# Edge sums with one-hots of 32 columns in four column groups of TensorE

## The reference

```python
m = x[src] * rel[edge_type]
m = concatenate([m[:half] @ W_in, m[half:] @ W_out])
deg = segment_sum(ones(e), dst); norm = 1 / maximum(deg, 1)
agg = segment_sum(m * norm[dst][:, None], dst)
out = tanh(agg + x @ W_loop + b)
```

## Time and profile before

| | |
|---|---|
| time, median of 3 runs (lowest, highest) | 1939.32 us (1937.36, 1941.78) |
| span of the profiled execution, first to last instruction | 1937.8 us |
| the execution's own time | not listed apart from its span; the span is 1.5 us below the median of the runs |
| PE busy | 1821.0 us, 94% of the span |
| POOL busy | 1322.3 us, 68% |
| DVE busy | 1248.8 us, 64% |
| ACT busy | 632.8 us, 33% |

### The profile page before, as it was taken

How to read it: one execution, slowest core, us unless ns; L and a number is a source line. 1 busy time by engine, 2 the same in 40 slices (tenths; PEclk the granted TensorE clock), 3 DMA queues, 4 the chain that set the end, 5 groups by cost and what they waited for, 6 DMA issues and landing times.

```text
span 1937.8 us, 28847 instructions
## 1 busy us (share of the span) xinstructions
PE 1821.0 (94%) x9176; PEld 1505.8 (78%) x9176; DVE 1248.8 (64%) x3345; ACT 632.8 (33%) x1552; POOL 1322.3 (68%) x1301
## 2 busy tenths in 40 slices
PE   2899899999899999999999789998899999999999
PEld 1567787887588888768888667876788888888998
DVE  6786465674855576486466645868765666654766
ACT  4452233343323333332333222332121211223443
POOL 6777777777777777777777757777777777770000
PEclk9999999999999999999999989999999999999999
DMA  9568666667776666687677856667766766661000
GB/s 274 177 198 258 203 191 206 186 202 222 243 209 199 204 194 198 208 249 214 193 218 220 274 190 229 190 200 224 229 182 215 209 199 200 190 181 17 15 28 28
DMA packets 194575, 371.44 MB, mean 192 GB/s; under 512 B 37993, under 2 KB 126095, under 8 KB 194430
## 3 DMA queue, kind: packets, MB, share of 16 engines
q0 software_dynamic: 77632, 223.91, 40.6%
q1 hardware_dynamic: 92228, 126.68, 19.9%
q10 hardware_dynamic: 24570, 19.04, 3.4%
HBM read 305.39 MB, written 64.95 MB: 191 GB/s over the span
## 4 chain that ended last, share of the span: by engine, by line
PE 80%; DVE 8%; issue 3%; DMA 3%; POOL 2%; SPq 2%; ACT 2%; DVEq 0%; ACTq 0%
PE ps_down L2765 16%; PE ps_hid L2753 16%; PE ps_seg L2629 15%; PE ps_kv L2662 5%; PE ps_x L2717 4%; PE ps_x L546 3%; PE ps_hid L3229 2%; PE ps_kv L3082 2%; POOL xg L959 2%; PE ps_hid L2682 1%; DVE xg L1055 1%; PE ps_kv L2795 1%; PE ps_down L2795 1%; DMA h_rows<-qT_all 1%; PE ps_hid L3220 1%
## 5 line engine op out<-in xcount | busy, mean ns | idle before, releaser
L959 POOL DMA_INDIRECT xg<-h_rows,idx_tab x416 | 437.2, 1051 | 143.3 <-issue 114.0
L906 POOL DMA_INDIRECT rg<-relation_rows,idx_tab x416 | 426.7, 1026 | 133.5 <-issue 126.1
L959 POOL DMA_INDIRECT xg<-xn_rows,idx_tab x416 | 423.4, 1018 | 131.9 <-issue 120.3
L2629 PE MATMUL ps_seg<-xg,hot 128*125 128x257 f32 x1664 | 414.8, 382 | 19.7 <-DVE xg L1055 19.5
L2753 PE MATMUL ps_hid<-hT,wff 128*128 128x250 f32 (+1 forms) x1920 | 368.3, 341 | 1.0 <-issue 0.8
L2629 PEld LDWEIGHTS ps_seg<-xg,hot 128*125 128x125 f32 x1664 | 305.3, 188 | 75.0 <-DVE xg L1055 19.2
L2765 PE MATMUL ps_down<-wff,gT 128*125 128x256 f32 x1600 | 363.6, 381 | 0.0
L2753 PEld LDWEIGHTS ps_hid<-hT,wff 128*128 128x128 f32 x1920 | 312.8, 189 | 37.9 <-issue 7.9
L1055 DVE TENSOR_TENSOR xg<-xg,rg 128x512 f32<-128x512 f32 x416 | 285.8, 687 | 70.8 <-DMA rg<-relation_rows,idx_tab 52.0
L2765 PEld LDWEIGHTS ps_down<-wff,gT 128*125 128x125 f32 x1600 | 295.2, 188 | 41.3
L2204 ACT ACTIVATE gT<-ps_hid,b1p 128x250 f32<-128x250 f32 (+1 forms) x480 | 177.8, 433 | 291.6 <-PE ps_hid L2753 291.5
(11 more groups left out here) (378 smaller groups left out, 2385.5 us busy)
## 6 DMA issues: line engine op xcount, KB each, us to landing
second_relation_rows<-rg SPq DMA_DIRECT2D x104, 512.0 KB, 4.1
rg<-second_relation_rows SPq DMA_DIRECT2D x104, 512.0 KB, 4.1
wff<-L_mix_W ACTq DMA_DIRECT2D x8, 1024.0 KB
rg<-relation_rows,idx_tab POOLq DMA_INDIRECT x416, 3.5
xg<-xn_rows,idx_tab POOLq DMA_INDIRECT x416, 3.2
xg<-h_rows,idx_tab POOLq DMA_INDIRECT x416, 3.6
h_rows<-qT_all SPq DMA_DIRECT2D x25, 112.0 KB
qrow<-h_rows ACTq DMA_DIRECT2D x25, 112.0 KB
```

The source lines that it names most:

```text
L906: pool.indirect_dma_start(rg[:, k, :], None, rel_d, bass.IndirectOffsetOnAxis(ap=idx_tab[:, step, 1:2], axis=0))\
L959: pool.indirect_dma_start(xg[:, k, 0:D], None, rows, bass.IndirectOffsetOnAxis(ap=idx_tab[:, step, 0:1], axis=0))\
L2629: ins = pe.matmul(ps_seg[u // UW % 2][0:T, 0:AW], hot[:, s % HOTS, :], xg[:, s % RING, :], start=s % WIN == 0, stop=s % WIN == WIN - 1)
```

## The change

One-hots become 32 columns wide in place of 125. The steps of a window are reordered so that step s of it goes to column group s modulo 4: two steps that follow each other in the sorted list share a group, and their destinations fit in 32 rows. PE takes a quad of four steps (two units) at a time: each step's product has 32 output rows, and the four go to the four groups of 32 columns of the array and of PSUM rows (`tile_position`). After the two quads of a window, the bank holds four blocks of 32 rows. DVE makes a placing one-hot (`placed`, from the new `place_tab`) and copies the bank to SBUF (`step_sums`; `copy_sums`, at the second unit of the next window); PE multiplies the two into the same bank (`place_sums`, after the next window's first quad), which puts each row where it stood before; then DVE does both adds, at the fourth unit instead of the third and fourth. `s_seg` moves by two units at a time, and a unit left over at a mark waits on PE for the next mark. The tables at the start gain `pair_pick`, `pair_first`, `place_tab` and a few more, and lose the step that shifted keys to their tile.

```diff
 STORE_AT = (2, 5)
 CUT = 112
 AHEAD = 6
+SPAN = 32
+COLS = P // SPAN
+QUAD = COLS
 
 
 
...
@@ -181,7 +184,10 @@
         xg = sb("xg", [EP, RING, AW])
         rg = sb("rg", [EP, RING, 2 * D])
         rg2 = rg[:, :, :].rearrange("p r (h d) -> p (r h) d", h=2)
-        hot = sb("hot", [EP, HOTS, T])
+        hot = sb("hot", [EP, HOTS, SPAN])
+        step_sums = sb("step_sums", [P, AW])
+        placed = sb("placed", [P, T])
+        place_tab = sb("place_tab", [P, WINS])
         iota_t = sb("iota_t", [EP, T])
...
+            pool.affine_select(out=pair_pick, in_=pair_pick, compare_op=ALU.not_equal, fill=1.0, base=0,
+                               pattern=[[-2, SCH // 2], [0, 2]], channel_multiplier=1)
...
+                            p(dve.tensor_copy(spread_steps(idx_tab[:, :, m]), by_groups(ps_tab[2 * m][0:EP, 0:STEPS2])))
...
@@ -1022,10 +1047,16 @@
                     self.rows = row, nc.s_assert_within((row < last_row) + row, min_val=0, max_val=last_row,
                                                         skip_runtime_bounds_check_because="one more only below the last")
 
+                def copy_sums(self, w):
+
+                    dve.tensor_scalar(placed[:, :], iota_t[:, :], place_tab[:, w:w + 1], None, ALU.is_equal)
+                    dve.wait_ge(s_seg, self.g * UNITS + (UW * (w + 1) + RU))
+                    dve.tensor_copy(step_sums[:, :], ps_seg[w % 2][:, 0:AW]).then_inc(s_cps, 1)
+
                 def add(self, w, m):
 
                     if m == 0:
-                        dve.wait_ge(s_seg, self.g * UNITS + (UW * (w + 1) + RU))
+                        dve.wait_ge(s_plc, self.g * WINS + w + 1)
                     dve.wait_ge(s_acc, (self.g * WINS + w) * 2 + (m + 3))
                     if self.scaled:
                         dve.wait_ge(s_sc, self.g * NB + self.scaled)
...
@@ -1041,10 +1072,11 @@
                         self.row_numbers(k // UW - 1)
                     at = k * UNIT
                     s = at % RING
-                    hs = at % HOTS
-                    dve.wait_ge(s_seg, g * UNITS + (k + 1 + RU - HOTS // UNIT))
-                    dve.tensor_tensor(hot[:, hs:hs + UNIT, :], iota_t[:, :].unsqueeze(1).broadcast_to([EP, UNIT, T]),
-                                      key_tab[:, at:at + UNIT].unsqueeze(2).broadcast_to([EP, UNIT, T]), ALU.is_equal)
+                    if at % QUAD == 0:
+                        hs = at % HOTS
+                        dve.wait_ge(s_seg, g * UNITS + (k + QUAD // UNIT + RU - HOTS // UNIT))
+                        dve.tensor_tensor(hot[:, hs:hs + QUAD, :], iota_t[:, 0:SPAN].unsqueeze(1).broadcast_to([EP, QUAD, SPAN]),
+                                          key_tab[:, at:at + QUAD].unsqueeze(2).broadcast_to([EP, QUAD, SPAN]), ALU.is_equal)
...
                     dve.tensor_tensor(m, m, r, ALU.mult).then_inc(s_msg, 1)
-                    if k % UW in (2, 3) and k > UW:
-                        self.add(k // UW - 1, k % UW - 2)
+                    if k > UW and k % UW == 1:
+                        self.copy_sums(k // UW - 1)
+                    if k > UW and k % UW == 3:
+                        for m in range(2):
+                            self.add(k // UW - 1, m)
...
                 def flush(self):
                     assert self.done == UNITS
+                    self.copy_sums(WINS - 1)
                     self.row_numbers(WINS - 1)
...
+            p(dve.tensor_scalar(row_i, part_i, SPAN - 1, None, ALU.bitwise_and))
...
+            p(dve.tensor_scalar(spread_steps(key_tab[:, :]), by_groups(ps_tab[1][0:EP, 0:STEPS2]), unsorted_f[:, 0:1], None, ALU.add))
+            p(dve.tensor_scalar(place_tab[:, :], ps_hid[0][:, 64:64 + WINS], row_in_span, None, ALU.add))
+            p.wait()
+            p(dve.tensor_scalar(over, place_tab[:, :], float(T), -float(T), ALU.is_ge, ALU.mult))
+            p.wait()
+            p(dve.tensor_tensor(place_tab[:, :], place_tab[:, :], over, ALU.add))
...
                     self.g, self.done = g, 0
 
                 def unit(self):
-                    u = self.done
+                    u, steps = self.done, range((self.done - 1) * UNIT, (self.done + 1) * UNIT)
                     self.done += 1
-                    if u % UW == 0:
-                        pe.wait_ge(s_acc, (self.g * WINS + u // UW) * 2 + 1)
+                    if self.done * UNIT % QUAD:
+                        return
+                    w = u // UW
+                    if u % UW == 1:
+                        pe.wait_ge(s_acc, (self.g * WINS + w) * 2 + 1)
                     pe.wait_ge(s_msg, self.g * UNITS + (u + 2 + RU))
-                    for s in range(u * UNIT, (u + 1) * UNIT):
-                        ins = pe.matmul(ps_seg[u // UW % 2][0:T, 0:AW], hot[:, s % HOTS, :], xg[:, s % RING, :],
-                                        start=s % WIN == 0, stop=s % WIN == WIN - 1)
-                    ins.then_inc(s_seg, 1)
+                    for s in steps:
+                        rows = slice(s % COLS * SPAN, (s % COLS + 1) * SPAN)
+                        ins = pe.matmul(ps_seg[w % 2][rows, 0:AW], hot[:, s % HOTS, :], xg[:, s % RING, :],
+                                        start=s % WIN < COLS, stop=s % WIN >= WIN - COLS, tile_position=(0, rows.start))
+                    ins.then_inc(s_seg, QUAD // UNIT)
+                    if u % UW == 1 and w:
+                        self.place_sums(w - 1)
+
+                def place_sums(self, w):
+
+                    pe.wait_ge(s_cps, self.g * WINS + w + 1)
+                    pe.matmul(ps_seg[w % 2][0:T, 0:AW], placed[:, :], step_sums[:, :], start=True, stop=True).then_inc(s_plc, 1)
+
+                def flush(self):
+                    assert self.done == UNITS
+                    self.place_sums(WINS - 1)
...
                 aside(8)
+                if (lay, gi) == (L - 1, NG - 1):
+                    edges.flush()
...
                         turn_sums(t + 1)
+                    if t and among(t - 1) == AMONG > among(t - 2):
+                        edges.flush()
...
+            pe.matmul(ps_hid[0][:, 64:64 + WINS], pick_pair, pair_places.rearrange("p c w -> p (c w)"), start=True, stop=True)
```

More of the change, by code:

```diff
@@ L280, in build @@
         spans = scratch(SCH, 4 * EP).rearrange("p (c t) -> p c t", c=4)
-        first, tile_of, base, place, bad, due = (scratch(SCH, 4) for _ in range(6))
+        both_first = scratch(SCH, 8)
+        first, pair_first = both_first[:, 0:4], both_first[:, 4:8]
+        tile_of, base, place, pair_place, bad, due = (scratch(SCH, 4) for _ in range(6))
         reached = scratch(SCH, 4 * (NT - 1)).rearrange("p (c t) -> p c t", c=4)
@@ L285, in build @@
         tile_row = scratch(1, WINS)
-        quad_first = scratch(SCH, SCH)
+        quad_first, pair_pick = (scratch(SCH, SCH) for _ in range(2))
+        row_i, row_in_span = scratch(P, 1).bitcast(I32), scratch(P, 1)
+        in_window, of_window = scratch(SCH, WIN), scratch(SCH, SCH // WIN)
+        pick_pair = scratch(SCH, P)
+        pair_places = scratch(SCH, 4 * (SCH // WIN)).rearrange("p (c w) -> p c w", c=4)
+        over = scratch(P, WINS)
         pair_a, pair_b = (flat_r[0:PAIR_ROWS, i * PAIRS:(i + 1) * PAIRS].bitcast(I32) for i in range(2))
@@ L357, in build @@
         s_seg = counted("segments_done", RU)
+        s_cps = sem("step_sums_copied")
+        s_plc = sem("step_sums_placed")
         s_acc = counted("acc_added", 3)
@@ L572, in start, with spread_steps, by_groups @@
                 eng.sem_inc(s, START.pop(id(s)))
+        def spread_steps(v):
+            return v.rearrange("p (w h j) -> p w h j", h=WIN // COLS, j=COLS)
+        def by_groups(v):
+            return v.rearrange("p (w j h) -> p w h j", h=WIN // COLS, j=COLS)
         def is_tile(t):
@@ L1900, in _ @@
             dve.wait_ge(s_const, 1)
-            p(dve.tensor_copy(part[:, :], part_i))
+            p(dve.tensor_copy(part[:, :], part_i[0:T]))
+            p(dve.tensor_scalar(row_i, part_i, SPAN - 1, None, ALU.bitwise_and))
+            steps_in = ident[0:SCH, 0:SCH].rearrange("p (w m) -> p w m", m=WIN)
+            p(dve.tensor_reduce(of_window, steps_in, AX, ALU.add))
+            p(dve.tensor_reduce(in_window, steps_in.rearrange("p w m -> p m w"), AX, ALU.add))
+            p.wait()
+            p(dve.tensor_copy(row_in_span, row_i))
+            p(dve.tensor_copy(pick_pair.rearrange("p (j r) -> p j r", j=COLS),
+                              in_window.rearrange("p (j h) -> p j h", j=COLS)[:, :, 0:1].broadcast_to([SCH, COLS, SPAN])))
             p(dve.tensor_copy(ramp_all, ramp_i))
@@ L1949, in _ @@
             fronts[0].norm(2)
-            keys = step_rows_f[:, 1]
-            p(dve.tensor_tensor(keys, keys, base.unsqueeze(2).broadcast_to([SCH, 4, EP]), ALU.add))
-            p.wait()
-            p(dve.tensor_scalar(dropped, keys, float(T), -float(T), ALU.is_ge, ALU.mult))
             for ch in (1, 3):
```

(12 more changed lines are left out.)

20 lines of the change are left out of this document (13 added, 7 removed).

## The result

The changed kernel takes 1971.62 us (median of four runs, 1969.44 to 1976.81); the kernel before, run beside it, takes 1938.34 (four runs, 1937.23 to 1941.78): ratio 1.0176, 95% interval 1.0153 to 1.0199. The forecast was 1922, faster.

A forecast was written before the change was run, and what follows sets the result against it. POOL was taken to bound the first layer and PE the second, POOL close behind. Terms -23 + 8 - 4 + 1.5 = -17.5 on a 1937.8 us span gave 1920, forecast median 1922; range 1900 to 2005, the forecast's own 1905 to 1945.

The forecast's parts named there:

- What bounds the kernel: First layer set by POOL, second by PE with POOL close behind; cheaper edge products can shorten only the second.
- The quad: Second layer's edge work on PE, with placing and switching: 151 us against 181, 30 saved, 23 of them counted.
- Full overlap: Rival: a step's two passes don't hold up other column groups on PE; about 1911 us, chance 0.23.
- the middle case: The forecast itself: a quad's four steps start near 0.22 us apart on PE; 1922 us, chance 0.42.
- The waits that come with it: Five new waits between DVE, PE and ring slots: nothing to 23 us, taken as 8 us more.
- The waits eat it: Rival: overlap as forecast, but DVE and PE run in lockstep, 43 us in place of 8; 1945 us, chance 0.13.
- (4): Fourth listed wait: ring slots come free by two units, the first of the two about 2.8 us later.
- (5): Fifth listed wait: PE leaves an odd unit for the next mark; no size of its own.
- POOL's contention: First layer's gathers, stretched by DVE's `hot`, end earlier as 113 us of it go: 0 to 13, taken as 4.
- Between the layers: One more copy and placing product on the way to the last sums: 1.5 us more, range nothing to 2.
- Tables at the start: Some ten small DVE instructions, about 2 us, and two on POOL, hidden by a wait of 5.44 us.
- The clock: PE's clock falling because PE idles at marks, named as counting also against full overlap; no size given.

The follow-up runs named there:

- even_split: The changed kernel with whole quads at PE's marks and only the second of a window's two adds one unit later, both in the second layer: 1925.22 us.
- same_group: The changed kernel with a quad's four steps going two and two to the same column group (output not the reference's): 1990.87 us.
- unplaced_adds: The changed kernel with all placing work done, but the adds read the unplaced sums and don't wait for the placing product (output not the reference's): 1936.30 us.
- no_placing: The changed kernel without placing one-hot, copy and placing product, adds at the third and fourth unit (output not the reference's): 1915.21 us.
- no_placing_even: no_placing with whole quads at the marks in the second layer (output not the reference's): 1907.24 us.
- kept_busy: even_split with two more unused products of 128 columns on PE ahead of each quad's wait for messages in the second layer: 1930.05 us.

## Why the prediction was wrong

*What bounds the kernel.* Right: the first layer's gathers take 1082 us in both kernels, though PE's edge work there is cheaper. POOL limits the gain: of the 29 us that the prediction allowed, the best kernel with the whole computation gains 12.5 (even_split, against 1937.75 beside it). In its profile the second layer's gathers and what follows take 761.6 us in place of 783.4, 21.8 less; its first layer takes 1090.1 in place of 1082.5 and gives 7.6 of that back.

*The quad.* A term of the sum mis-sized: 1.09 us taken, 0.57 measured, which is the lower bound of 0.435 and 0.135 until the next product starts; with the 0.1 at the entry, switching costs some 0.23 a quad, 104 x 0.23 = 24 us a layer, where I took 15. (The prediction's upper end for full overlap, 0.87, does not follow from its terms: 0.435 and three starts of 0.11 make 0.77. Nothing hung on it.) From 1155 to 1437 the edge products fall from 94.11 us to 50.5, 32.42 in quads and 18.11 in placing products.

The mechanism for the middle case, in which a step's second pass holds up the next group's first, failed: in the quad shown, four passes start within 21 ns and the other four 0.24 us later. In same_group, too, two start together at each turn; they are taken to be of two groups (the trace does not name the group), so steps that the kernel lists one behind the other were not started so. Whether the compiler or the engine put them in another order isn't seen. The Trainium skill, TensorE: Matmul & The Clock Gate, Part 3, states program order for the starts; taken for the order of the steps in the kernel, this trace does not agree. Its 2.38 for three groups was the better guide: here 1.74 us of serial passes stand against 0.57, 3.05 times for four groups. The Trainium skill, TensorEngine Tiling (Array Packing), section Tiling Modes, has the array drained at a change of mode; the time lost at both ends of a quad agrees with that.

This error was in the kernel's favour. The rival *Full overlap* had the mechanism and gave 1911; measured is 1971.6.

*The waits that come with it: "I take 8".* **This is the step that failed.** All five waits were listed, and priced as if they were independent and mostly hidden, because DVE idles a third of the second layer. Idle time did not help, since the adds stand on a loop: quad, placing product, adds, messages, quad. Before, the first add stood at the third unit of the next window and waited for the last unit of its own; now it stands at the fourth unit and waits for a product behind the quad of the first two. With an odd mark that quad comes a mark late. The runs put 35 us on the wait (unplaced_adds), 21 on the rest of placing and 41 on the odd marks, not to be added, since 33 us need both. The price bound of 23 us, "a copy of 0.45 in each of 52 windows waited out by PE", was at the wrong place: PE's placing products wait 1.0 us in all for the copies and their weight loads 12.2; DVE's adds wait 69.3, and POOL pays.

*The waits eat it.* This rival had the direction and the loop, with 43 us from too small a mechanism (one copy and one product a window) and on top of the smaller overlap; it gave 1945, range 1940 to 1957. Against Full overlap's 1911 the measured price is 60 us.

*POOL's ring*, (4) and (5) of the list, had no price of its own. "POOL gives at most its 12.8 us of waits" was a bound on the gain; the loss, to 53.6, was not bounded at all.

*Small terms.* POOL's contention, 4 us: the first layer's gathers take 1082.5 us before and 1082.7 after, so nothing is gained; 10.3 us are in the second, swallowed by the waits. The term counted the `hot` that leaves DVE (171.1 us become 59.3) and not the placing work that comes (43.5 us of copies, 30.7 of one-hots, and the products). Without that work the first layer's gathers take 1075.0 (no_placing) and 1070.5 (no_placing_even), against 1081.5 to 1090.1 in the six kernels that share the change's first layer, so 7.5 to 12 us were there to gain and the placing took them back. In unplaced_adds, where the work is done and the adds don't wait for it, they take 1081.2: it is not that wait; which part of the work it is stays open. Between the layers 1.5: nothing. Tables at the start: hidden. The clock: 0.91 from 1155 to 1437, 51 us of it at 1.2 GHz where there were none. The prediction named this. It costs something on the path where a quad stands behind a wait (0.90 us for 0.57, above); what it costs in the sum no run separates, and kept_busy and no_placing_even speak against it as the main cause.

What stays open: how the 21 us of placing divide between DVE and PE, what the lower clock costs, and whether a longer ring would give the odd marks' 41 us back, which was not tried.

## What to carry to other kernels

A cheaper product is worth what its chain lets through: before pricing the product, write the loop of waits around it (who frees the buffer, who waits for that, at which mark) and count how many units each engine may run ahead, before and after. An added wait on a loop was not hidden here by the idle time of the engine that waits, because that idle time is the wait of the same loop. A small change of when PE works, whole quads at the marks, turned 1.8% slower into 0.6% faster, and beyond that the gathers are the bound.

## What the runs showed that was not expected

Four fp32 products of 257 columns in four column groups start 5 to 8 ns apart in each pass and take 0.57 us together, where their eight passes over the whole array take 8 x 0.2175 = 1.74; two and two in one group take 1.00. A weight load of 32 columns is recorded at 105 to 109 ns, one of 125 at 188 to 194 on average. And the mean granted clock of PE fell from 0.990 to 0.950 of the span when PE became less busy (94% and 88%), without a loss of the whole that any run could pin on it.
